# Four conditioned sequence layers on one core: where the MLP residuals, the first fills, a layer norm and the last C product are done

## What is computed

```
# layer 2 (layer 0 is the same without mask and without g1, g2)
h = LN(x);  q, k, v = h @ Wqkv + bqkv              # 16 heads x 16
x = x + g1 * (softmax(mask(q k^T / 4)) v @ Wo + bo)
x = x + g2 * (gelu(LN(x) @ W1 + b1) @ W2 + b2)
# layer 3: 512 inner channels, 32 states, both directions
xc = silu(conv(h @ Win));  dt = softplus(...);  B, C = xc @ Wx
state = state * exp(dt * A) + dt * B * xc          # for each channel and state, over 512 positions
y = sum over states(state * C) + D * xc
x = x + g1 * (y_forward + y_backward) * silu(z) @ Wout
x = x + g2 * (silu(LN(x) @ w1) * (LN(x) @ w2)) @ w3
```

## Time and profile before

| | before |
|---|---|
| median of three runs | 6402.1 us (6397.88 to 6406.35) |
| profiled execution | 6410.27 us |
| its span in the trace | 6408.5 us |
| TensorE busy | 5860.4 us (91%) |
| TensorE weight load busy | 3032.5 us (47%) |
| VectorE busy | 4471.8 us (70%) |
| ScalarE busy | 4212.1 us (66%) |
| GpSimd busy | 2649.7 us (41%) |

### The profile page before, as it was taken

One profiled execution on the slowest core, in us unless ns is written; L12 is line 12 of the kernel. 1 busy time (PEld: TensorE's weight loads), 2 busy tenths in 40 slices (PEclk: granted clock), 3 DMA queues, 4 the chain that ended last, 5 costly groups with the idle time before them and its releaser, 6 DMA issues. The chain is left out here.

```text
span 6408.5 us, 77313 instructions
## 1 busy us (share of the span) xinstructions
PE 5860.4 (91%) x28624; PEld 3032.5 (47%) x28624; DVE 4471.8 (70%) x4944; ACT 4212.1 (66%) x6876; POOL 2649.7 (41%) x1962
## 2 busy tenths in 40 slices
PE   8999999999999998989988888889898888988897
PEld 5444445555555554444444444444444444444444
DVE  5656654444434435566664998989898998989897
ACT  3344445444455544434435989979898998979896
POOL 0000002222222221000000977959595886959596
PEclk8999999999999999999998999999999999999999
DMA  4313120000000002231231102010101102010100
GB/s 130 46 31 60 31 50 22 1 1 1 1 1 1 1 1 56 40 56 32 42 61 32 42 19 59 25 51 29 47 30 39 37 21 56 29 48 30 47 29 19
DMA packets 152791, 216.14 MB, mean 34 GB/s; under 512 B 24289, under 2 KB 91194, under 8 KB 152162
## 3 DMA queue, kind: packets, MB, share of 16 engines
q1 hardware_dynamic: 152418, 211.21, 14.2%
HBM read 146.61 MB, written 30.44 MB: 28 GB/s over the span
## 5 line engine op out<-in xcount | busy, mean ns | idle before, releaser
L2334 DVE TENSOR_TENSOR_SCAN l__h<-l__decay,psum 128x1024 f32<-128x1024 f32 x1024 | 2275.3, 2272 | 80.9 <-ACT l__decay L1930 28.7
L2318 POOL TENSOR_TENSOR l__hc<-l__h,l__c_rep 128x1024 f32<-128x1024 f32 x1024 | 2039.4, 2005 | 189.5 <-DVE l__h L2334 124.8
L1930 ACT ACTIVATE l__decay<-l__dt_rep,l__a_neg 128x511 f32<-128x511 f32 x2048 | 1425.3, 784 | 15.0 <-DVE l__h L2334 14.8
L1937 PEld LDWEIGHTS psum<-ident,l__dtx_B 128*128 128x128 f32 x8192 | 893.0, 142 | 1106.5 <-DVE l__h L2334 685.3
L1937 PE MATMUL psum<-ident,l__dtx_B 128*128 128x128 f32 x8192 | 1132.9, 282 | 260.2 <-ACT l__dtx_B L1915 181.1
L1915 ACT ACTIVATE l__dtx_B<-l__dtx_T,l__b_T 128x512 f32<-128x512 f32 x1792 | 1268.8, 781 | 38.3 <-PEq L2429 35.8
L2403 PE MATMUL psum<-l__hc,l__gather 128*64 128x512 f32 x4096 | 1117.3, 624 | 12.5 <-POOL l__hc L2318 12.0
L1029 ACT ACTIVATE l__probs<-psum 128x1024 f32<-128x1024 f32 x512 | 515.5, 1026 | 609.2 <-PE psum L1092 603.5
L197 POOL TENSOR_SCALAR l__ln_var_eps<-l__ln_mean_var 128x4 f32<-128x4 f32 x64 | 18.1, 282 | 2112.3 <-DVE l__ln_mean_var L183 2111.7
L691 DVE TENSOR_REDUCE l__row_max<-psum 128x1 f32<-128x512 f32 x1024 | 659.0, 686 | 275.0 <-PE psum L706 272.8
L1404 POOL TENSOR_SCALAR l__probs<-l__probs,l__rec 128x512 f32<-128x512 f32 x512 | 351.3, 699 | 938.0 <-DVE l__rec L1400 937.9
(11 more groups left out here) (165 smaller groups left out, 6772.1 us busy)
## 6 DMA issues: line engine op xcount, KB each, us to landing
l__c_rep<-l__c_dram SPq DMA_DIRECT2D x512, 128.0 KB, 2.8
l__dt_rep<-l__dt SPq DMA_DIRECT2D x128, 256.0 KB, 5.1
l__parts_dram<-l__parts SPq DMA_DIRECT2D x64, 384.0 KB, 3.5
l__q_stack<-l__parts_dram SPq DMA_DIRECT2D x192, 128.0 KB, 6.2
l__k_stack<-l__parts_dram SPq DMA_DIRECT2D x192, 128.0 KB, 8.8
l__w<-in_l_w SPq DMA_DIRECT2D x6, 1024.0 KB, 7.6
in_mod_w<-in_mod_w SPq DMA_DIRECT2D x1, 4608.0 KB, 17.2
out_x<-x_sb SPq DMA_DIRECT2D x8, 512.0 KB, 3.2
```

Source lines behind the costliest of these rows:

```text
L1930: nc.scalar.activation(decay[:, i % DECAYS, s, 1:T], dt_rep[:, w, c, s, 1:T], ACT.Exp, scale=a_neg[:, g, c, s:s + 1]).then_inc(S["decay"], 1)
L1937: last = nc.tensor.transpose(bx_psum(i)[:, s, t * P:(t + 1) * P], dtx_B[:, (k + 1) % 2, t, 2 * c + s, :, :].rearrange("p j d -> p (j d)"), ...
L2318: nc.gpsimd.tensor_tensor(hc[:, i % HCS, :, :], h[:, i % HS, :, :], c_of_i, ALU.mult).then_inc(S["hc"], 1)
L2334: nc.vector.tensor_tensor_scan(both(h[:, i % HS, :, :]), both(decay[:, i % DECAYS, :, :]), both(bx_psum(i)), 0.0, ALU.mult, ALU.add).then_ ...
```

## The change

Narrow layers:

- The MLP residual of batches 0 to 5 leaves VectorE. ScalarE copies banks 6 and 7 to `res_tmp` at the end of the batch (`mlp_out`), GpSimd adds the bias, multiplies by the gate (layer 2) and adds to x (`mlp_res`) in the next batch. The last two batches keep it on VectorE. The columns of the condition are copied behind tile 30 instead of 26.
- The 24 early tiles use a ring of four banks throughout (before: 20 of them, then two banks). The 40 late tiles and the row transposes share a ring of three banks (6, 0, 1); each place of it waits for whatever used the bank three places before. The two pairs of banks of the transposed scores swap their order.

State-space layer:

- All eight batches stand in one block, with counts per batch in place of the barrier.
- The MLP residual of a batch goes behind scan 1 of the next one and uses the fourth buffer of `hc`; GpSimd's fourth product and TensorE's first sums wait for it.
- Fill 0 stands ahead of the wait for the last product of the MLP, fill 1 ahead of the down projection.
- The next batch's layer norm statistics come behind scan 64 (`mid_stats`), its reciprocal root on GpSimd there, its bias behind scan 68; the normalisation itself goes from VectorE to ScalarE, behind its last decays but one.
- The product with C of the last unit is made by VectorE (`hc_last`).
- x of the batch before is stored after the fourth load of C rows.

The diff, cut to its core:

```diff
-    RESIDUAL_AT = LEAD + 2
+    CUR_AT = LEAD + 6
...
-        RING0, SOLO = 4, LEAD - 4
-        max_bank = lambda n: bank[n % RING0] if n < SOLO else bank[n % 2]
-        pair = lambda n: psum[:, 2 + 2 * (n // 2 % 2):4 + 2 * (n // 2 % 2), :]
+        RING0 = 4
+        LATE_RING = (6, 0, 1)
+        rows_slot = lambda gg: min(GT * (gg + 1) + 2, TILES - 1) - LEAD + gg
+        late_slot = lambda n: n - LEAD + sum(n > GT * (gg + 1) + 2 for gg in range(1, NG))
+        slot_bank = lambda slot: bank[LATE_RING[slot % len(LATE_RING)]]
+        max_bank = lambda n: bank[n % RING0] if n < LEAD else slot_bank(late_slot(n))
+        pair = lambda n: psum[:, 4 - 2 * (n // 2 % 2):6 - 2 * (n // 2 % 2), :]
...
-            if n >= SOLO:
-                pe.wait_ge(*S.at("max_taken", done + n - 1))
-            elif n >= RING0:
+            if n >= RING0:
...
-        def mlp_residual(dve, x_b):
-            residual(nc, dve, S, bank[6:8], b2[:, :], gates.rows[:, 1, :] if gated else None, tmp, x_b, 1,
-                     "down_filled")
+        def mlp_residual(pool, x_b):
+            over = lambda row: row.unsqueeze(1).broadcast_to([P, 2, D])
+            for k in range(2):
+                done = RES_STEPS * k - 2 * RES_STEPS
+                half, x_half = tmp[:, k, :, :], x_b[:, 2 * k:2 * k + 2, :]
+                pool.wait_ge(*S.at("mlp_out", k - 1))
+                nc.gpsimd.tensor_tensor(half, half, over(b2[:, :]), ALU.add).then_inc(S["mlp_res"], 1)
+                pool.wait_ge(*S.at("mlp_res", done + 1))
+                if gated:
+                    nc.gpsimd.tensor_tensor(half, half, over(gates.rows[:, 1, :]), ALU.mult).then_inc(S["mlp_res"], 1)
+                    pool.wait_ge(*S.at("mlp_res", done + 2))
+                nc.gpsimd.tensor_tensor(x_half, x_half, half, ALU.add).then_inc(S["mlp_res"], 1)
...
+            if S.batch:
+                mlp_residual(pool, x[:, b - 1, :, :])
...
-                if n == RESIDUAL_AT:
-                    if S.batch:
-                        S.batch -= 1
-                        mlp_residual(dve, x[:, b - 1, :, :])
-                        S.batch += 1
+                if n == CUR_AT:
...
-                    make_max_rows(dve, bank[6], n // GT - 1)
+                    make_max_rows(dve, slot_bank(rows_slot(n // GT - 1)), n // GT - 1)
...
+            if S.batch:
+                dve.wait_ge(*S.at("mlp_res", 0))
...
+            if b + 1 < JOINED:
+                for k in range(2):
+                    act.wait_ge(*S.at("down_filled", k + 1))
+                    nc.scalar.activation(tmp[:, k, :, :].rearrange("p t n -> p (t n)"), bank[6 + k],
+                                         ACT.Copy).then_inc(S["mlp_out"], 1)
...
+            def slot_free(pe, slot):
+                of = slot - len(LATE_RING)
+                rows = sum(rows_slot(gg) < of for gg in range(1, NG))
+                if rows + 1 < NG and rows_slot(rows + 1) == of:
+                    pe.wait_ge(*S.at("max_part2", rows + 1))
+                elif of >= 0 or S.batch:
+                    pe.wait_ge(*S.at("max_taken", of - rows + 1))
+
             def late_scores(n):
-                if n >= LEAD + 2 or S.batch:
-                    pe.wait_ge(*S.at("max_taken", n - LEAD - 1))
+                if n == LEAD and S.batch:
+                    pe.wait_ge(*S.at("mlp_out", -1))
+                slot_free(pe, late_slot(n))
                 scores(pe, n)
             def max_rows(gg):
                 pe.wait_ge(*S.at("max_taken", GT * (gg + 1) - LEAD))
-                if gg == 1 and S.batch:
-                    pe.wait_ge(*S.at("res", 0))
-                if gg > 1:
-                    pe.wait_ge(*S.at("max_part2", gg - 1))
-                max_transposes(pe, gg, bank[6])
+                slot_free(pe, rows_slot(gg))
+                max_transposes(pe, gg, slot_bank(rows_slot(gg)))
...
-    STATS_AFTER, SCALED_AFTER = UNITS - 5, UNITS - 3
+    STATS_AFTER, BIAS_AFTER, COLUMNS_AFTER, SCALED_AFTER = UNITS // 2, UNITS // 2 + 4, UNITS - 3, UNITS - 4
...
+        mlp_tmp = hc[:, HCS - 1, :, :].rearrange("p s (t n) -> p s t n", n=D)
...
-                residual(nc, dve, S, bank[6:8], None, gates.rows[:, 1, :], tmp, x_end, 1, "down_filled")
+                if not begin:
+                    mlp_residual(dve, x_end)
...
+            def first_fill(i):
+                groups = UNITS // IC if end else 1
+                pe.wait_ge(*S.at("dtxB", (OPS - 1) * groups))
+                pe.wait_ge(*S.at("dtxB_pool", groups))
+                pe.wait_ge(*S.at("dtxT", 2 * IC))
+                fill_bx(i)
...
+                if begin:
+                    first_fill(0)
                 pe.wait_ge(*S.at("prod", HC))
+                if begin:
+                    first_fill(1)
...
+            residual(nc, dve, S, bank[6:8], None, gates.rows[:, 1, :], mlp_tmp, x_b, 1, "down_filled")
...
+                if i == HCS - 1 and S.batch:
+                    pool.wait_ge(*S.at("res", 0))
...
+                if i == RESIDUAL_AFTER and S.batch:
+                    dve.wait_ge(s_dt_rep[IC - 1], dt_rep_of(b))
+                    S.batch -= 1
+                    mlp_residual(dve, x[:, b - 1, :, :])
+                    S.batch += 1
+                if i == RESIDUAL_AFTER:
+                    nc.vector.tensor_copy(cur[:, :], mod[:, b, mod0:mod0 + n_mod]).then_inc(S["cur"], 1)
...
+                if i == STATS_AFTER and begin:
+                    for t in range(TT):
+                        nc.vector.bn_stats(mid_st[:, t, :], x[:, b + 1, t, :]).then_inc(S["stats"], 1)
+                    dve.wait_ge(*S.at("stats", TT))
+                    for t in range(TT):
+                        nc.vector.bn_aggr(mid_mv[:, t, :], mid_st[:, t, :]).then_inc(S["aggr"], 1)
+                if i == BIAS_AFTER and begin:
+                    dve.wait_ge(*S.at("rstd", 1))
+                    nc.vector.scalar_tensor_tensor(mid_bias[:, :], mid_mv[:, :, 0], -1.0, mid_rs[:, :], ALU.mult,
+                                                   ALU.mult).then_inc(S["norm_bias"], 1)
...
+                if i == UNITS - 1:
+                    dve.wait_ge(*S.at("scan", UNITS))
+                    dve.wait_ge(*S.at("c_rep", 16 * NJ * (UNITS // IC)))
+                    dve.wait_ge(*S.at("y_sum", UNITS - HCS))
+                    nc.vector.tensor_tensor(hc[:, i % HCS, :, :], h[:, i % HS, :, :], c_of(i),
+                                            ALU.mult).then_inc(S["hc_last"], 1)
...
+                if i == SCALED_AFTER and begin:
+                    act.wait_ge(*S.at("norm_bias", 1))
+                    act.wait_ge(*S.at("bx_filled", UNITS - IC - FILLED))
+                    for t in range(TT):
+                        nc.scalar.activation(norm.xn[:, t, :], x[:, b + 1, t, :], ACT.Identity,
+                                             bias=mid_bias[:, t:t + 1], scale=mid_rs[:, t:t + 1]).then_inc(S["xn"], 1)
...
+                if i >= 2 and w == 0 and g == 0 and S.batch:
+                    pe.wait_ge(*S.at("res", 0))
+                if i == UNITS - 1:
+                    pe.wait_ge(*S.at("hc_last", 1))
...
-            for b in range(B):
-                begin = b + 1 < B
-                x_of_b = x[:, bass.ds(b, 1), :, :].rearrange("p b t d -> p (b t) d")
-                with nc.Block() as block:
...
-                            if i == STATS_AFTER and begin:
-                                ahead.stats(nc, dve, b + 1, 0)
-                            if i == SCALED_AFTER and begin:
-                                ahead.scaled(nc, dve, b + 1, 0)
...
-                nc.all_engine_barrier(sems_to_clear=S.range)
+            with nc.Block() as block:
+
+                @block.sync
+                def _(sp):
+                    for b in range(B):
+                        S.batch = b
+                        sync_batch(sp, b)
+
+                @block.gpsimd
+                def _(pool):
+                    for b in range(B):
+                        S.batch = b
+                        gpsimd_batch(pool, b)
+
+                @block.vector
+                def _(dve):
+                    for b in range(B):
+                        S.batch = b
+                        vector_batch(dve, b)
```

337 lines of the change are left out of this document (191 added, 146 removed).

## The result

| | before | after |
|---|---|---|
| median | 6400.2 us (four runs) | 6241.1 us (four runs, 6236.5 to 6245.2) |
| ratio | | 0.975, 95% interval 0.9733 to 0.9767 |
| span of the profiled execution | 6408.5 us | 6241.4 us |
| forecast | | 6203 us, range 6170 to 6290 |

A forecast was written before the change was run, and what follows sets the result against it. ScalarE was taken to bound the state-space unit loop, TensorE/VectorE waits the narrow layers. Gains of 116 (narrow) and 83 (state-space, seven batches) sum to 199 us: 6410.3 becomes 6211, the median 8 lower, 6203 us; range 6170 to 6290.

The forecast's parts named there:

- What bounds the kernel: State-space unit loop: ScalarE sets the pace at 0.61 us per instruction; VectorE work is free while it can catch up.
- Narrow layers, 116 us: Layers 0 and 2: residual off VectorE and three banks for late score matmuls gain 116 us, between 42 and 140.
- The lower bound: Layer 2 stretch, 27th maximum to last: gain at least VectorE's own residual time, 4.2 us; 9.3 us was forecast.
- GpSimd's part: Narrow-layer residual: GpSimd's additions and products 1.0 us each, ScalarE's copies at most 0.67 us each, beside other work.
- End of the unit loop less the middle: State-space batch: moving statistics and normalisation gains 4.7 us at the loop's end; statistics mid-loop stall ScalarE 0.85 us.
- Behind the last scan: State-space layer, last scan to convolution: 6.2 us instead of 9.2, so 3.0 us gained per batch, 0 to 3.5.
- The handover: Between state-space batches: ScalarE restarts 5.1 us earlier, 2.3 to 5.1, with fill 0 early and no block end.
- The residual in the loop, 0 us: State-space residual behind scan 1: 2.8 us plus the GpSimd lock on VectorE, no ScalarE stall, caught up by unit 35.
- my bound of 4.0: State-space residual, worst case: each x addition waits a full GpSimd product, 2 x 2.0 us; ScalarE then stalls 2.8 us.
- Rival 2: State-space layer: low clock again behind the last scan and both x additions locked out; 6251 us, chance 0.15.
- Rival 1: Narrow layers: three banks bring nothing, TensorE's order sets the pace; narrow gain 42 us, 6277 us in all, chance 0.17.
- rival 5: Narrow layers: late matmuls wait for the maximum directly before, steps take 1.1 us; slower, 6465 us, chance 0.04.

## Why the prediction was right, and where it was wrong

- **What bounds the kernel.** Right for the unit loop: with nothing held, it stayed at ScalarE's pace, and work on VectorE was free (statistics at scan 96) while it could fall behind.
- **Narrow layers, 116 us: measured 115 to the first scan.** That the sum came out is luck in part. In the stretch forecast, the twelve middle batches gained 39.7 us in layer 0 (49 forecast; the batch that I read, 35.6 us, was one of the longer ones, the mean is 35.1) and 49.3 in layer 2 (56), the four others 12.8 (11). The remaining 13 us came outside it, 9.0 of them in layer 2 between the last maximum of a batch and the first of the next; what brought them was not tested. The split was wrong as well. The lower bound (4.2 us in layer 2) took the residual alone at VectorE's time and gave the stop of TensorE to the ring. The run with two banks shows 7.1 us for the residual alone and 1.1 more for the ring. The stop and the half clock behind it go when the residual leaves VectorE; with the ring alone they stayed, 3.54 us and a clock of 0.50.
- **GpSimd's part.** Its additions take 1.27 us each, not 1.0, ScalarE's copies 0.60; in the batch shown nobody waits for them.
- **End of the unit loop less the middle, 4.7 - 0.85 = 3.85 us: measured 3.85 (26.9 / 7).** The stall of 0.85 us beside the four additions measured 0.9 (145.3 less 144.4), and goes when the statistics are moved. Here mechanism and size were right.
- **Behind the last scan, 3.0 us.** The start of the convolution moved 1.2 us on the mean (8.48 to 7.27; the batch that I read had 9.2), and it was the wrong mark. I left out that VectorE itself has 1.2 + 5.3 + 0.8 us to do there, and that the convolution's start does not decide anything: TensorE does. Its half clock is gone, and in the batch shown its twelve projections start 4.0 us behind the last scan in place of 7.0. To the last product of the MLP the gain is 2.2 us on the mean. The last product's move brings nothing of it, as its run shows; that the normalisation's move brings it is what is left, and no run undid that move by itself.
- **The handover, 5.1 us for ScalarE's restart: measured 5.2.** From the last product to scan 0 it is 6.2 us (8.97 to 2.75), of which scan 0's earlier place against ScalarE is 1.0. Nothing of it was tested apart. In the table 2.2 + 6.2 = 8.4 us stand against 8.1: that agreement is luck, since one part fell short and the mark at scan 0 gave the other too much.
- **The residual in the loop, 0 us: measured 4.1 to 5.5 us per batch from scan 0, 32 us in all; counted from ScalarE's decay 2, 3.1 to 4.5 us, 25 in all.** This is the step that failed. It had the right mechanism, "2.8 us plus the GpSimd lock", priced the lock at 1.2 us, and concluded "no stall". The lock took 1.81 + 1.08 = 2.9 us, between that and my bound of 4.0. I had set the first addition against GpSimd's scaling and the second against product 0. In fact the scaling was just over, product 0 started 0.05 us ahead of the first addition, and product 1 met the second. That makes ScalarE wait 2.13 us for scan 2. The bound was too low as well, 2.8 us, since I had no price for TensorE's pause, after which fills and sums ran at half clock and the scans waited for them: 1.0 to 2.4 us more per batch. What the forecast said of the residual itself holds: with GpSimd waiting and the clock at 1.00, ScalarE does not stall.
- **Rival 2** (the handover gives it back, 6251 us) came nearer to the time than the forecast. Its first half, half clock behind the last scan, did not happen; its second did. Of the Trainium skill, SBUF — State Buffer, section Who interferes with whom, two sentences bear on it: a VectorE instruction with two SBUF inputs contends with GpSimd's reads, and a copy in its fast mode takes the shared pair as well, the one that comes second being blocked for the other's whole instruction. The runs agree in the length: 1.87 us for a one-column addition, 1.94 for a twelve-column copy, and 0.69 for the full addition and 0.17 for the copy where GpSimd was held. Whether the copy ran in that fast mode, no trace shows. The row that the forecast held against the rule is a TENSOR_SCALAR with one wide input, so the additions are the first case here with two.
- **Rival 1** (the ring brings nothing) is refuted at 30 us, 6270.9 against 6241, though with two banks the narrow layers still gained 79 us to the first scan (3516.1 to 3436.9), not the 42 that it gave them; **rival 5** did not occur: the steps became shorter, 2.83 us for four.

## What to carry to other kernels

Before work is moved onto an engine "because it is free there", look at what runs beside it: an addition of two SBUF tiles on VectorE next to a stream of GpSimd products waits up to one product each, whatever its own size. The cure is to let GpSimd wait: it has the slack, and one moved wait gave back 20 of the 32 us. Price a stop of TensorE with the slow stretch that may follow it, and look at several batches: behind the same 3.39 us pause the clock fell in five of seven. And cut a trace at the engine that sets the pace, here at ScalarE's decays and not at scan 0, or a shift between two engines looks like a cost.

## What the runs showed of the hardware

- The lock between VectorE and GpSimd lasts until GpSimd's instruction ends, whatever VectorE's is: a one-column addition took 1.87 us and a copy of twelve columns 1.94 us beside products of 2.0 us. Scans, with one input in SBUF and one in PSUM, took 2.2 to 2.3 us beside the same products.
- After pauses of 4.37, 3.39 and 2.62 us, TensorE's next fills and sums took up to twice as long (1.94 us for eight fill matmuls that otherwise take 1.09; granted clock 0.57 and 0.54 behind the first two). Not after each: behind the 3.39 us pause the clock stayed at 1.00 in two of seven batches, behind the 2.62 us pause in three of seven.
- With unchanged narrow layers the first scan of the state-space layer lay between 3401.0 and 3411.8 us from one profiled execution to the next.
